# Moving one shared iteration ahead of the routed tiles, pacing the row scatters, and ranks by running sums in a fused ViT tower

## The reference, cut to what matters

```python
def _L1_ffn_ref(x, router_w, w_gate, w_up, w_down, ws_gate, ws_up, ws_down, sg_w, sg_b):
    ...
    probs = jax.nn.softmax(x @ router_w, axis=-1)
    gates, idx = jax.lax.top_k(probs, TOPK_ROUTED)
    gates = gates / jnp.sum(gates, axis=-1, keepdims=True)
    ...
h = _layernorm(h + _L1_ffn_ref(h, ...), axis=-1)
```

## Time and profile before

| | |
|---|---|
| median of 3 runs | 950.01 us (946.84 to 950.54) |
| span of the profiled execution, first to last instruction | 943.4 us |
| what lies around the span, median less span | 6.6 us |
| TensorE matmul busy | 835.2 us, 89% |
| VectorE, ScalarE, GpSimd busy | 58%, 49%, 43% |
| mean granted TensorE clock | 0.955 of 2.4 GHz |

### The profile page before, as it was taken

The page is one execution under the profiler, slowest core; times in us unless marked ns, Lnnn a source line. Parts: engine busy times, 40 slices in busy tenths (PEclk is TensorE's granted clock), DMA queues, the critical chain, the costliest instruction groups (busy, mean ns, idle before and its releaser), DMA issues. The chain is left out here.

```text
span 943.4 us, 20900 instructions
## 1 busy us (share of the span) xinstructions
PE 835.2 (89%) x7535; PEld 751.7 (80%) x7535; DVE 543.5 (58%) x1467; ACT 459.1 (49%) x1148; POOL 406.1 (43%) x471
## 2 busy tenths in 40 slices
PE   6999999999997999979999889988799159999985
PEld 5989998899985777768999867777589159899885
DVE  2145565455665888873834258988774012666563
ACT  1146555555552778843455357777361001455441
POOL 3434454334554434442422267778504720244451
PEclk9999999999999999987999979999899659999998
DMA  9710101111010321217000026332001211233161
GB/s 302 246 48 21 30 26 35 39 30 30 25 35 15 52 41 28 29 16 181 1 1 1 1 61 136 66 67 42 5 2 43 77 34 29 76 98 101 61 190 41
DMA packets 103492, 55.76 MB, mean 59 GB/s; under 512 B 67200, under 2 KB 94192, under 8 KB 103392
## 3 DMA queue, kind: packets, MB, share of 16 engines
q1 hardware_dynamic: 98384, 43.63, 19.0%
q0 software_dynamic: 3792, 7.84, 2.4%
q10 hardware_dynamic: 1216, 2.95, 1.0%
HBM read 29.81 MB, written 13.97 MB: 46 GB/s over the span
## 5 line engine op out<-in xcount | busy, mean ns | idle before, releaser
L931 POOL TENSOR_TENSOR attn_prob<-attn_prob,attn_recip 100x432 f32<-100x432 f32 x64 | 58.6, 915 | 75.1 <-DVE attn_recip L1310 74.8
L1872 POOL DMA_INDIRECT results<-moe_hid_shared x43 | 41.4, 962 | 92.0 <-ACT moe_hid_shared L2089 92.0
L450 POOL TENSOR_TENSOR attn_prob_x<-attn_prob,attn_recip 100x864 f32<-100x864 f32 x32 | 52.7, 1646 | 52.6 <-DVE attn_recip L759 52.6
L2064 ACT ACTIVATE moe_silu<-psum 128x384 f32<-128x384 f32 x36 | 17.6, 488 | 86.2 <-remote 45.4
L1596 ACT ACTIVATE mlp_hid<-psum,columns 128x384 f32<-128x384 f32 x72 | 38.1, 579 | 41.4 <-PE psum L96 41.4
L2244 DVE TENSOR_TENSOR moe_hid_shared<-psum,moe_silu 128x384 f32<-128x384 f32 x36 | 19.9, 554 | 59.8 <-remote 36.5
L1060 PEld LDWEIGHTS psum<-attn_prob_t,attn_values 108*64 108x64 f32 x1024 | 39.2, 142 | 12.3 <-ACT attn_prob_t L1179 7.8
L2479 PE MATMUL psum<-embed_w_tok,embed_patches 128*128 128x192 f32 x216 | 38.5, 338 | 10.0 <-DMA embed_w_tok<-in_tok_w 6.0
L1060 PE MATMUL psum<-attn_prob_t,attn_values 108*64 108x36 f32 x1024 | 41.5, 228 | 5.5 <-ACT attn_prob_t L1179 3.0
L1033 PE MATMUL psum<-attn_keys_a,attn_q_a 128*64 128x288 f32 x256 | 45.7, 436 | 0.0
L2479 PEld LDWEIGHTS psum<-embed_w_tok,embed_patches 128*128 128x128 f32 x216 | 36.5, 197 | 11.5 <-DMA embed_w_tok<-in_tok_w 6.0
(11 more groups left out here) (470 smaller groups left out, 2834.0 us busy)
## 6 DMA issues: line engine op xcount, KB each, us to landing
embed_patches<-in_x SPq DMA_DIRECT2D x8, 768.0 KB, 23.2
sorted_rows<-mlp_pad_zeros SPq DMA_DIRECT2D x1, 4214.0 KB, 16.8
moe_hid_shared<-sorted_rows SPq DMA_DIRECT2D x43, 98.0 KB
attn_v<-attn_v_tok SPq DMA_DIRECT2D x16, 216.0 KB
attn_values<-attn_v_tok SPq DMA_DIRECT2D x96, 27.0 KB
side_raw_a<-in_w_gu_dram SPq DMA_DIRECT2D x8, 288.0 KB, 3.3
side_raw_b<-in_w_gu_dram SPq DMA_DIRECT2D x16, 144.0 KB, 3.4
h_rows<-results SPq DMA_DIRECT2D x6, 288.0 KB, 5.3
```

The lines of the kernel that those rows point to most:

```text
L450: nc.gpsimd.tensor_tensor(prob_x[k % 2][:, :, :, :], prob[k % 3][:, :, :].rearrange("p h (a n) -> p h a n", a=1) .to_broadcast([QP, HEADS, ...
L931: nc.gpsimd.tensor_tensor(pr, pr, recip[k % 2][:, :].rearrange("p (h a) -> p h a", a=1) .to_broadcast([QP, HEADS, SEQ]), ALU.mult).then_in ...
L1872: nc.gpsimd.indirect_dma_start(out=results, out_offset=bass.IndirectOffsetOnAxis(ap=x_in[j % x_ring][:, D:D + 1].bitcast(U32), axis=0), in ...
```

## The change

It does three things.

1. Five shared iterations stand ahead of the routed tiles and one (number 5, "last") behind them. late_order and done_order say in which order results are loaded and iterations finished. The last iteration is no longer finished tile by tile: finish_last, last_pow and normalise_last are gone, and GpSimd's and VectorE's queues at the end are in another order. The waits of the second late iteration (all_placed on VectorE) go with it.
2. Each of the 36 row scatters first waits for a step of the shared products (shared_step). Step v is, in iteration v // 9 + 1, its product r, or, for the last three, a tile of the combine of the iteration before. Scatter k waits for step 2 + 32k // 35.
3. The ranks: GpSimd adds up "both" tile by tile into "earlier" (add_up, 18 sums of 128x8), and one matmul over ones takes the place of 18. The tile "over" now lies in the memory of "earlier".

```diff
-    sh, iters, ahead = HID // P, TOK // MW, 4
+    sh, iters, ahead = HID // P, TOK // MW, 5
...
-    late_order = [0, *range(ahead, iters), *range(1, ahead)]
+    last = iters - 1
+    late_order = [0, last, *range(1, ahead)]
+    done_order = [0, 1, 2, last, 3, 4]
...
-        both = sb("both", [P, NT + 1, EXPERTS])
+        both, earlier = sb("both", [P, NT + 1, EXPERTS]), sb("earlier", [P, NT + 1, EXPERTS])
...
         def hid_of(i):
-            return hid_shared[i % 2 if i < ahead else (i + 1) % 2]
+            return hid_shared[(i + ahead) % 2 if i < ahead else 1]
...
         @block.gpsimd
...
+            def add_up(t):
+                pool.wait_ge(S["both_ready"], t // 3 + 2)
+                pool.wait_ge(S["earlier_ready"], t + 1)
+                nc.gpsimd.tensor_tensor(earlier[:, t + 1, :], earlier[:, t, :], both[:, t, :], ALU.add
+                                        ).then_inc(S["earlier_ready"], 1)
+
+            def shared_step(v):
+                i, r = divmod(v, sh + 3)
+                if r < sh:
+                    pool.wait_ge(S["hid_ready"], sh * (i + 1) + r + 1)
+                else:
+                    pool.wait_ge(S["combined"], 3 * i + r - sh + 1)
...
+            nc.gpsimd.memset(earlier[:, 0, :], 0.0).then_inc(S["earlier_ready"], 1)
+            for t in range(NT):
+                add_up(t)
...
             for s, rows_ in enumerate((h_rows, rows_2)):
                 pool.wait_ge(S["slot_ready"], s + 1)
                 for t in range(NT):
+                    shared_step(2 + 32 * (NT * s + t) // (2 * NT - 1))
                     nc.gpsimd.indirect_dma_start(
...
             add_pair(0)
-            add_pair(ahead)
-            add_pair(ahead + 1)
-            for i in range(1, ahead):
+            add_pair(last)
+            for i in (1, 2, 3):
                 add_pair(i)
                 out_pow(i - 1)
-            out_pow(ahead - 1)
-            out_pow(ahead)
-            for t in range(3):
-                last_pow(t)
+            add_pair(4)
+            out_pow(last)
+            out_pow(3)
+            out_pow(4)
 
         @block.tensor
...
             def count():
+                pe.wait_ge(S["earlier_ready"], NT + 1)
...
                 nc.tensor.matmul(rank_ps, before_p[:, :], both[:, :, :], start=True, stop=False)
-                for t in range(NT):
-                    n = NT - t
-                    last = nc.tensor.matmul(rank_ps[:, t + 1:, :], ones[:, :],
-                                            both[:, t:t + 1, :].to_broadcast([P, n, EXPERTS]),
-                                            start=False, stop=(t == NT - 1))
-                last.then_inc(S["counted"], 1)
+                nc.tensor.matmul(rank_ps, ones[:, :], earlier[:, :, :], start=False, stop=True
+                                 ).then_inc(S["counted"], 1)
...
-            silus(ahead)
-            for c in range(sh):
-                silus(ahead + 1, [c])
-                if 1 <= c <= ahead:
-                    normalise(c - 1)
-            normalise(ahead)
+            silus(last)
+            for i in done_order:
+                normalise(i)
...
             for c in range(4):
-                multiply(ahead, c)
+                multiply(last, c)
             add_results(0)
             finish(0)
-            multiply(ahead, 4)
-            add_results(ahead)
-            multiply(ahead, 5)
-            add_results(ahead + 1)
-            for c in range(sh):
-                multiply(ahead + 1, c)
-                if 1 <= c + 1 < ahead:
-                    add_results(c + 1)
-                    finish(c + 1)
-            combine(ahead)
-            finish(ahead)
-            combine(ahead + 1, [0])
-            finish_last(0)
-            combine(ahead + 1, [1])
-            normalise_last(0)
-            finish_last(1)
-            combine(ahead + 1, [2])
-            normalise_last(1)
-            finish_last(2)
-            normalise_last(2)
+            multiply(last, 4)
+            add_results(last)
+            multiply(last, 5)
+            for i in (1, 2):
+                add_results(i)
+                finish(i)
+            combine(last)
+            finish(last)
+            for i in (3, 4):
+                add_results(i)
+                finish(i)
```

59 lines of the change are left out of this document (21 added, 38 removed).

## The result

In the first comparison the changed kernel takes **911.34 us** (median of 4 runs, 908.41 to 913.77), the kernel before 949.22 (4 runs, 946.84 to 950.54): a ratio of 0.963, with a 95% interval of 0.959 to 0.966. That is 37.9 us faster, where 32.2 was forecast. The range (911 to 930) just holds it. The profiled execution took 908.41 us, its span is 906.7.

The account below looks back on a forecast made before the run. TensorE was taken to bound the stage except for a 36.8 us hole, ascribed to dense GpSimd scatters delaying ScalarE and VectorE. Gains 3.4 + 18.5 + 10.3 = 32.2 us: 950.0 - 32.2 = 917.8 us, range 911 to 930.

Parts of the forecast that it names:

- (a): Counting of ranks: one matmul over ones instead of 18, TensorE waiting 0.3 us for running sums; gain 3.4 us.
- (b): One more shared iteration ahead of the routed tiles: gate_up(4) and one down add 16.3 us there.
- (c): Row scatters paced 1.63 us apart close TensorE's 36.8 us hole, less 2 us; with the added iteration, gain 18.5 us.
- for the pace: What the scatters' wider spacing would still cost between down(0) and the first turned rows: 2 us, bounds 0 to 13.
- R2: Rival: the scatters are not the cause and the hole stays at 36.8 us; 952.6 us, chance 0.07.
- R1: Rival: scatters 1.63 us apart still too dense, all 13 us stay; 929 us, chance 0.16 with what lies between.
- R3: Rival: price per scatter, not density; 36 at 1.36 us each cost 49 us; 965 us, slower, chance 0.05.
- the size of the hole: gate_up(2) to down(1) takes 47.3 us, the same work in iteration 3 10.5 us: TensorE loses 36.8 us.
- no wait of ScalarE's silu over 3 us: Sign of being right: between the first and last row scatter, no silu wait exceeds 3 us.
- The other signs of being right: Scatters about 1.6 us apart; down(0) to turned rows 61-65 us; counting under 1.5; clock 1.00; end 25-29 us, released by GpSimd.
- (d): The end: last normalisation at T0 (first load of results) + 26.6 instead of + 36.9 us; gain 10.3 us.
- The 6.6 us between span and median: Profiled span 943.4 against median 950.0 of the kernel before; the difference was taken as unchanged by the change.

Follow-up runs that it names:

- e6: Kernel before with only the new counting (running sums, one matmul over ones); dense scatters and four iterations ahead stay: 942.06 us against 946.17 for the kernel before.
- e7: Changed kernel without scatter waits for shared steps; five memsets ahead of each of the first 18 scatters, last 18 back to back: 938.18 us, kernel before 948.18.
- e10: Changed kernel with eight small GpSimd memsets ahead of each row scatter instead of the waits for shared steps: 911.51 us, kernel before 945.70.
- e3: Kernel before with two small GpSimd memsets ahead of each row scatter, nothing else changed: 912.42 us against 909.54 for the kernel before.
- e8: Changed kernel with one GpSimd power ahead of each row scatter instead of the waits for shared steps: 916.56 us, kernel before 910.89.

## Why the prediction was right, and where not

**(a) Counting: right.** 3.4 forecast, 3.27 in the profile, and with the old count put back 3.29 us are lost again. TensorE waited 0.24 us for the running sums; three sums took 0.93 us in the timeline.

**(b) and (c): right on the chips where there is a hole, with what sets it off, and blind to the chips.** 81.72 to 61.18 is 20.5 us where 18.5 was forecast; the step that was mis-sized is the 2 us "for the pace", which cost nothing. The hole was 36.8 by subtraction of two iterations, and the kernel before without it is shorter by 36.8 us in just that length. That on such a chip it depends on the density of the scatters is now shown and no longer only inferred, though not in one kernel and not on one chip: e6 and e7 keep the density, wholly or in part, and keep 37.0 and 26.3 us of hole, whatever else of the change they have; e10 takes the density away without the coupling, and it is gone. So R2 falls, R1's "1.63 may be too dense" falls but for the 0.9 us of one combine, and R3 (a price per scatter) falls with e10, in which all 36 go out beside steps on TensorE's path at no cost.

What the prediction got wrong was silent in it: "the size of the hole" was treated as a property of the kernel. On chips 12, 0 and 8 it isn't there, and then (b) stands alone at +16.25 and, measured on chip 0, the change is 0.3% slower. No rival said so. R2's 952.6 looked like the case "not the cause", but the case "no hole to close" has another sum: 906.6 + 16.3 - 3.4 - 10.3 = 909.2 for the span. That the forecast held is in this respect luck: the comparison was made where the hole was.

One reading in it was also off: ScalarE's 45.4 us are not all late, since some 7 of them are the usual wait at a down. For the same reason its sign "no wait of ScalarE's silu over 3 us" could not come out: this wait reaches 7.1 us or more in every profile, stalled or not. The other signs of being right came out.

The Trainium skill (SBUF — State Buffer, "Who interferes with whom") says that TensorE and ScalarE never wait on anyone at SBUF. The trace of e6 has ScalarE up to 17.0 us late at a time, in dense scatters; TensorE only waits there for VectorE. That is no proof against the rule, since the way may be another one, and no run here shows which; but a forecast that had leaned on it would have come to 952.6.

**(d) The end: right in kind, 1.6 us short.** T0 + 36.9 became + 28.2 against + 26.6 forecast; the eight profiles with this order of the end have + 27.2 to + 28.2. Three instructions of VectorE are longer than their rows: "var_eps" with 1.41 us and once more with 0.97 (0.17 elsewhere), and a sum with 1.86 (0.75), each begun while GpSimd makes a pair sum. In the row that the prediction read, VectorE's add had begun first (906.09) and the pair sum beside it (906.26) took 1.86 us. So it let this contention lengthen the pair sums, which had time to spare. Now the pair sums begin first (878.23 against 878.24, 879.95 against 880.10) and stay at 1.40. It is VectorE, the engine that sets the end, which is held, some 3.1 us in this profile. The statistics of 5 then end near + 21.3 instead of + 19.6, and the 2.1 us for each of the last two iterations is as forecast. The loads of results start 3.4 us behind the gate products instead of 2.6. The nine profiles with five iterations ahead have 2.56 to 3.49, the five with four all 2.56 to 2.59, so the change may have a part in it; what lengthens it in some of them is not shown.

**The sum.** Against the span the forecast was 911.2, and 906.7 came. Of the 4.5 us, 3.5 lie ahead of the stage: it starts at 680.14 instead of 683.68, in code that the change doesn't touch. Over the profiles of this study it starts between 680.0 and 685.9, for kernels that are the same up to there. The pace gives 2.0, the routed tiles 0.6; the end takes back 1.6, the later T0 0.9 and the count 0.1, and another 0.1 lies between the count and down(0). The last 1.1 come from the stretch behind the last normalisation, where the prediction put the last stores at nothing. The three terms themselves give 3.27 + 20.54 + 8.68 = 32.5 us against the 32.2 of the forecast; that they meet so closely is partly luck, since 2.0 too much for the pace and 1.6 too much for the end cancel.

Against the medians 917.8 was forecast and 911.34 came, 6.5 us apart: 2.0 more than between the spans. The 6.6 us between span and median were not what lies around the span, which is 1.7 to 1.9 us in every execution that has both. The profiled execution of before took some 945.2 us by this, less than any of the four runs, and that of after was 2.9 us under its median.

**Still open:** whether it is the chip or the occasion, what in it makes the difference, whether the recording has a part in it, and by which path the starts are delayed. The late engines show "remote" or "issue", which names no releaser, and no kernel here took the path apart (fewer bytes in each row, or fewer rows in each scatter, weren't tried). The unchanged after was measured on only one chip with the hole; that its own runs of up to seven at 1.27 us do no harm but for 0.9 us in one combine rests on that one.

## What to carry to other kernels

Before a stall is explained, have the same kernel profiled on a second chip: a hole of 37 us in which engines wait for "remote" or "issue" with their inputs ready may be there on one chip and not on the next, and a fix for it is paid for on the others. Check in the timelines who is late before you blame an engine: a wait may be that of an engine whose input was late. Where such a hole shows beside a long stream of indirect scatters from GpSimd that has time to spare, spread the stream, by whatever GpSimd can do in between or by waits on steps of the work beside it: the first gives an even distance, the second gives a lull just when somebody is late. If a fix moves work to the front as cover, price it without the stall too: here 16.25 us in for 10.25 out.

## What the runs showed of the hardware

- On chips 9, 10, 1 and that of the first comparison, scatters of 128 rows at one per 1.27 us go with late starts of ScalarE (up to 19.8 us, before) and VectorE (up to 12.9 us, e6), from some 10 us into the stream until its end; TensorE and GpSimd are not late themselves. On chips 12, 0 and 8 the same stream at the same DMA share (0.23) delays nobody.
- At 1.45 us the starts are up to 5.3 us late, at 1.55 none is; a lull of 2.6 us behind 12 dense scatters is followed by some 10 us without a delay.
- On the first four chips the trace holds 106 to 450 of the 576 records of the landings of these scatters, on the other three all 576.
- From the start of the last row scatter to the first turned rows takes 4.7 us where that scatter is what is late (764.31 to 768.97 in e3, 777.12 to 781.84 in e8).
- GpSimd spends 0.30 us between two scatters that follow each other, and 0.16 if memsets stand between, so that the first 0.14 us of them are free: 2 memsets made 1.27 into 1.32 us, 5 into 1.45, 8 into 1.55. With a power of 0.57 us between, it is 0.20, the scatter itself grows from 0.96 to 1.04, and the distance is 1.83.
- A VectorE instruction that starts while GpSimd adds 128x576 may last 0.97 to 1.97 us instead of 0.17 or 0.75, and GpSimd's own stays at 1.40 to 1.43; where VectorE's add started first, GpSimd's pair sum took 1.86.
